# A fused Mamba-2 and Hadamard-FFN layer: the preparation stage's work moved into batch 0's own order

## What is computed

```python
xn = _layernorm(x)
# attention part: a Mamba-2 block on xn, and its own residual
zxbcdt = xn @ w_in                       # 512 -> z 1024, xBC 1280, dt 16
xBC = silu(causal_conv4(xBC) + conv_b)   # -> xh, B, C
y = ssd(xh * dt, dt * A, B, C) + xh * D  # state-space scan over the rows
y = y * silu(z)
y = y * rsqrt(mean(y * y) + EPS) * norm_w
mamba = xn + y @ w_out
# feed-forward part: gate, Hadamard transform of 2048, down
hidden = silu(xn @ W1.T) * (xn @ W3.T)   # 512 -> 2048
hidden = fwht(hidden)                    # / sqrt(2048)
ffn = hidden @ W2.T                      # 2048 -> 512
out = x + mamba + ffn
```

## Time and profile before

| | us |
|---|---|
| median of 3 runs | 1034.17 (1034.06 to 1037.31) |
| profiled execution | 1032.72 |
| its span, first to last instruction | 1030.8 |
| preparation, to the first projection | 0 to 111.3 |
| batch 0 | 111.3 to 357.9 |
| batches 1, 2, 3 | to 582, 806 and 1028 |

### The profile page before, as it was taken

How to read it: one execution, slowest core, us unless ns; L and a number is a source line. 1 busy time by engine, 2 the same in 40 slices (tenths; PEclk the granted TensorE clock), 3 DMA queues, 4 the chain that set the end, 5 groups by cost and what they waited for, 6 DMA issues and landing times.

```text
span 1030.8 us, 13120 instructions
## 1 busy us (share of the span) xinstructions
PE 925.2 (90%) x4924; PEld 464.5 (45%) x4926; DVE 649.1 (63%) x1096; ACT 384.1 (37%) x637; POOL 296.4 (29%) x182
## 2 busy tenths in 40 slices
PE   1027879998899999999999999999999999999997
PEld 1013334454454544555544444555544445555543
DVE  3997788778875275666754276766762565766631
ACT  3548455634432233623322234522321234442300
POOL 1962020434520020345410020544400111654400
PEclk9999899999999999999999999999999999999999
DMA  8448656754642153543622343643532433455123
GB/s 297 188 163 307 213 152 196 236 174 120 204 138 82 60 166 102 170 128 93 174 83 62 106 141 104 193 128 99 131 93 62 152 97 102 133 145 130 64 72 92
DMA packets 95103, 143.10 MB, mean 139 GB/s; under 512 B 7744, under 2 KB 46272, under 8 KB 91456
## 3 DMA queue, kind: packets, MB, share of 16 engines
q1 hardware_dynamic: 77120, 114.73, 36.2%
q10 hardware_dynamic: 17920, 27.53, 9.1%
HBM read 120.47 MB, written 21.76 MB: 138 GB/s over the span
## 4 chain that ended last, share of the span: by engine, by line
PE 76%; DVE 11%; DMA 5%; ACT 3%; issue 3%; SPq 1%; ACTq 0%; DVEq 0%
PE ps L434 49%; PE ps L592 16%; PE ps L564 3%; DMA arena<-w_in 2%; DMA arena<-w1t 2%; PE ps L550 2%; DVE arena L933 2%; DVE arena L348 2%; DVE arena L347 2%; PE ps L556 2%; PE ps L496 2%; PE ps L536 1%; DVE arena L973 1%; ACT arena L696 1%; PE ps L444 1%
## 5 line engine op out<-in xcount | busy, mean ns | idle before, releaser
L434 PE MATMUL ps<-xh,arena 128*128 128x512 f16 x1600 | 493.8, 383 | 15.5 <-DVE arena L973 9.0
L434 PE MATMUL ps<-xl,arena 128*128 128x512 f16 x800 | 306.5, 383 | 0.0
L434 PEld LDWEIGHTS ps<-xh,arena 128*128 128x128 f16 x1600 | 160.0, 100 | 207.2 <-issue 21.4
L1110 POOL TENSOR_TENSOR arena<-arena 128x512 f16<-128x512 f32 x64 | 82.5, 1290 | 317.5 <-ACT arena L736 317.5
L592 PE MATMUL ps<-arena 128*128 128x512 f16 x768 | 169.8, 379 | 0.0
L1116 POOL TENSOR_TENSOR arena<-arena 128x2048 f32<-128x2048 f32 x16 | 58.0, 3627 | 285.4 <-DMA arena<-cs_rows 285.4
L973 DVE SCALAR_TENSOR_TENSOR arena<-ps,cw,arena 128x511 f32<-128x511 f32 (+2 forms) x120 | 89.6, 749 | 52.0 <-ACT arena L726 50.1
L434 PEld LDWEIGHTS ps<-xl,arena 128*128 128x128 f16 x800 | 78.9, 99 | 89.3 <-issue 3.5
L592 PEld LDWEIGHTS ps<-arena 128*128 128x128 f16 x768 | 74.4, 98 | 88.0 <-issue 0.7
L736 ACT ACTIVATE arena<-arena 128x512 f16<-128x512 f32 x64 | 40.3, 630 | 167.8 <-DVE arena L994 167.8
L434 PE MATMUL ps<-wo_hi,arena 128*128 128x512 f16 x256 | 78.8, 379 | 0.0
(11 more groups left out here) (155 smaller groups left out, 1108.8 us busy)
## 6 DMA issues: line engine op xcount, KB each, us to landing
arena<-w_parts SPq DMA_DIRECT2D x214, 256.0 KB, 2.7
w_parts<-arena SPq DMA_DIRECT2D x66, 256.0 KB, 2.3
arena<-cs_rows ACTq DMA_DIRECT2D x16, 1024.0 KB, 6.0
arena<-ecs_rows ACTq DMA_DIRECT2D x24, 256.0 KB, 7.4
arena<-w_in SPq DMA_DIRECT2D x4, 1160.0 KB, 17.7
arena<-w_in SPq DMA_DIRECT2D x18, 256.0 KB, 3.7
arena<-x SPq DMA_DIRECT2D x4, 1024.0 KB, 6.5
arena<-w2t SPq DMA_DIRECT2D x1, 4096.0 KB, 16.4
```

The lines of the kernel that those rows point to most:

```text
L434: ins = nc.tensor.matmul(out_ap, lhs(i, a), rhs(i, c), start=(i == 0 and s == 0), stop=(i == n - 1 and s == 2))
L1110: nc.gpsimd.tensor_tensor(hid_lo[:, i, :], hs[i % 2], hid_hi[:, i, :], ALU.subtract).then_inc(hid_l.sem, 1)
```

## The change

There is no preparation stage. Each batch has its own order, and batch 0's holds what was prepared, as items of its own:

- `w_in`, W1 and W3 come from the host cut into tiles (each tile a contiguous block, in batch 0's order). All eighteen tiles of w_in are loaded once, at the start, into what is later the hidden buffers, and are split from there.
- The scale of w_in is two scales: one from the first four tiles and dt's columns, one (G1S) from the other fourteen.
- W1 and W3 are squared in four rounds: KA is the squaring (W1 on ACT, W3 on POOL, in four pieces each), K the column sum on PE and a maximum on DVE, KS the scale.
- W2 comes from the host with its rows shuffled, and the transform is two matmul passes: F with one sign matrix (16 matmuls, ACT squares the input and copies the result out, SP stores it as w2_mid) and, after the norm W2S, H with another (16 matmuls through PSUM bank 4, then split by ACT and DVE straight into the buffers from which G reads). W1's and W3's columns are shuffled alike. F stands between the up tiles, H between the last up tiles and the down tiles. W2's raw tiles lie in the hidden buffers.
- WOL, WOQ, WOS and WOH load, square, scale and split W_out, XL loads the next batch's x, HL starts the load of w2_mid.
- After w_in, raw tiles have six buffers in place of two (the two of before and the four buffers of W2's parts), and a load is issued eight tiles ahead.
- x of batch 0 is loaded first, in four pieces, and normalised by DVE. Constants are loaded from ACT's queue. A scale is four instructions in place of eight.
- The last chunk's N, V and W use bank 5 alone.

```diff
-RAW, PARTS, W2R = 2, 5, 4
+PARTS, W2R = 5, 4
+CONV_ORDER = [B_TILE, C_TILE] + list(range(QE))
+G1_PIECES = ((4, 8), (8, 12), (12, 16), (16, 18))
+RING = (("1", 0), ("3", 0), ("1", 1), ("3", 1), ("1", 2), ("3", 2), ("1", 3), ("3", 3))
+NRING = 5
+RAWS = 6
+RAW_LEAD = 8
+FIRST = ("B G1S C C0 DT C1 Z0 SUM C2 KA0 Z1 C3 K0 KA1 Z2 WOL C4 K1 KA2 Z3 C5 K2 KA3 Z4 C6 K3 KS Z5 C7 Z6 E0 Z7 F0 F1 "
+         "A0").split()
+FIRST_AT = ([("WOQ", q, q // 2 + 1) for q in range(8)] + [("WOS", 0, 6)] + [("WOH", q, q // 2 + 7) for q in range(8)] +
+            [("XL", 0, 14), ("HL", 0, 28), ("W2S", 0, 29)] +
+            [("F", m, 4 * (m // 2) - 2 + m % 2) for m in range(2, JF)] + [("H", j, 30 + j) for j in range(JF)])
...
         def load_raw(sp, p):
 
-            sp.wait_ge(w_lo.sem, w_lo.at(0, p - RAW))
-            sp.dma_start(raw[p % RAW], weight_tile(STREAM[p])).then_inc(d_raw[p % RAW], 16)
+            q = p - N_FRONT
+            if q >= RAWS:
+                sp.wait_ge(w_lo.sem, w_lo.at(0, p - RAWS))
+            elif q < 2:
+                sp.wait_ge(w_lo.sem, w_lo.at(0, q))
+            sp.dma_start(raws[q % RAWS].rearrange("p k m -> p (k m)"), weight_tile(STREAMS[0][p])).then_inc(d_raw[q % RAWS], 16)
...
+            for t in range(NC):
+                sp.dma_start(xraw[:, t, :], x[0, t * P:(t + 1) * P, :]).then_inc(d_x0[t], 16)
...
+                        if b == 0 and N_FRONT <= p + RAW_LEAD < NT:
+                            load_raw(sp, p + RAW_LEAD)
...
+                    elif kind == "H":
+                        if i + W2R < JF:
+                            load_h(sp, i + W2R)
+                        sp.wait_ge(evac.sem, evicted(0, (kind, i)))
+                        sp.dma_start(w2_parts[i].rearrange("p (a d) -> p a d", a=2), w2s[i % W2R]).then_inc(d_w2st[i % W2R], 16)
...
+                    elif kind == "G1S":
+                        pe.wait_ge(scale_g0, 1)
+                        pe.wait_ge(sq_g1, len(G1_PIECES))
+                        pe_norm(pe, SQ_G1, SQ_G1 + 5, sum_g1)
+                    elif kind == "K":
+                        pe.wait_ge(scale_g1, 1)
+                        pe.wait_ge(ones16_ok, 1)
+                        if i > 0:
+                            pe.wait_ge(k_read, i)
+                        pe.wait_ge(k_act, i + 1)
...
+                        pe.wait_ge(k_pool, 4 * (i + 1))
...
+                    elif kind == "F":
+                        to = claim((kind, i))
+                        pe.wait_ge(d_had, 16)
+                        pe.wait_ge(d_w2r[i // 2], 32)
+                        nc.tensor.matmul(to, had_a, w2_raw[i], start=True, stop=True).then_inc(f_done, 1)
...
+                    elif kind == "H":
+                        if i == 0:
+                            pe.wait_ge(scale_w2, 1)
+                        else:
+                            pe.wait_ge(evac.sem, evicted(0, ("H", i - 1)))
+                        pe.wait_ge(d_h[i % W2R], 16 * (i // W2R + 1))
+                        nc.tensor.matmul(bank(4), had_b, h_raw[i % W2R], start=True, stop=True).then_inc(h_done, 1)
...
+                    elif kind == "F":
+                        act.wait_ge(d_w2r[i // 2], 32)
+                        if i > 0:
+                            act.wait_ge(sq_w2, i)
+                        square(w2_junk, w2_raw[i], SQ_W2 + i, sq_w2)
+                        act.wait_ge(f_done, i + 1)
+                        if i == 0:
+                            act.wait_ge(xt_done.sem, xt_done.at(0, MC - 1))
+                        elif i >= 2:
+                            act.wait_ge(d_mid[i % 2], 16 * (i // 2))
+                        nc.scalar.activation(w2m[i % 2], tile_bank(0, (kind, i)), ACT.Copy).then_inc(f_out_ok, 1)
...
+                    elif kind == "WOQ":
+                        act.wait_ge(d_wo, 16)
+                        if i > 0:
+                            act.wait_ge(sq_wo, i)
+                        nc.scalar.activation(wo_junk, wo_raw[:, i, :], ACT.Square, scale=nw[:, i:i + 1],
+                                             accum_out=row_sq[:, SQ_WO + i:SQ_WO + i + 1]).then_inc(sq_wo, 1)
...
+                    elif kind == "H":
+                        dve.wait_ge(had_hi, i + 1)
+                        nc.vector.scalar_tensor_tensor(out=w2s[i % W2R][:, 1, :], in0=bank(4), scalar=f_had[:, 0:1],
+                                                       in1=w2s[i % W2R][:, 0, :], op0=ALU.mult, op1=ALU.subtract).then_inc(evac.sem, 1)
...
+                    elif kind == "KA":
+                        n = RING_AT["3", i]
+                        pool.wait_ge(d_ring[n % NRING], 16 * (n // NRING + 1))
+                        if i > 0:
+                            pool.wait_ge(k_sums, i)
+                        for s in range(4):
+                            piece = slice(s * TILE, (s + 1) * TILE)
+                            nc.gpsimd.tensor_tensor(sq_pool[:, piece], ring[n % NRING][:, piece], ring[n % NRING][:, piece],
+                                                    ALU.mult).then_inc(k_pool, 1)
```

More of the change, by code:

```diff
@@ L168, in build @@
         row = view(1)
-        yh, yl = cut(view(E // 2, FP16), QE), cut(view(E // 2, FP16), QE)
-        assert used[0] >= STAGED
-        raw = [cut(view(KD * P), KD) for _ in range(RAW)]
+        w2_junk = view(D // 2, BF16)
+        yh = cut(view(E // 2, FP16), QE)
+        yl_at = used[0]
+        yl = cut(view(E // 2, FP16), QE)
+        raw_at = used[0]
+        raw = [cut(view(KD * P), KD) for _ in range(2)]
         parts = [view(KD * P, FP16) for _ in range(PARTS)]
@@ L472, in _ @@
-            pe_dt_proj(pe, 0)
-            pe.wait_ge(sq_ok_w, SQ_WO)
-            nc.tensor.matmul(bank(2)[:, 0:KD], ones, row_sq[:, 0:SQ_W2], start=True, stop=True)
-            nc.tensor.matmul(bank(2)[:, KD:KD + QE], ones, row_sq[:, SQ_IN:SQ_WO], start=True, stop=True).then_inc(sums_w, 1)
-            pe_cumsums(pe, 0)
-            def column_sums(i):
-                for squares, done in ((sq_act, w13_sq_act), (sq_pool, w13_sq_pool)):
-                    pe.wait_ge(done, i + 1)
-                    for n in range(HF // L):
-                        ins = nc.tensor.matmul(bank(4 + n), ones16, squares[i % 2][:, n * L:(n + 1) * L],
-                                               start=(i == 0 and squares is sq_act),
-                                               stop=(i == KD - 1 and squares is sq_pool), skip_group_check=True)
-                ins.then_inc(w13_sums, 1)
@@ new lines, in _, with square @@
+            act.dma_start(hads[:], consts[:, 4 * P:6 * P]).then_inc(d_had, 16)
+            def square(junk, w, column, done):
+                nc.scalar.activation(junk, w, ACT.Square, accum_out=row_sq[:, column:column + 1]).then_inc(done, 1)
+            act.wait_ge(guards, 1)
+            nc.scalar.activation(first[:], row_sq[:, SQ_G0 + 3:SQ_G0 + 4], ACT.Square)
+            act.wait_ge(d_g0, 48)
+            square(sq_act[:, 0:2 * TILE], at(raw_at, 2 * TILE), SQ_G0, sq_g0)
+            act.wait_ge(sq_g0, 1)
@@ new lines, in _ @@
+            dve_ln(dve, steps, 0)
+            dve.wait_ge(ln_ok.sem, ln_ok.at(0, 0))
+            for t in range(NC):
+                nc.vector.tensor_scalar(xraw[:, t, :], xraw[:, t, :], rstd[:, t:t + 1], nmr[:, t:t + 1], ALU.mult,
+                                        ALU.add).then_inc(xn_ok.sem, 1)
+            dve.wait_ge(sum_g0, 1)
+            to_scale(IN0, bank(FREE_BANK)[:, 0:4], ALU.add)
+            dve.nop().then_inc(scale_g0, 1)
+            dve_xl(dve, 0, (0, 1))
+            steps.step(nc.vector.tensor_scalar(f_in[:], inv[:, IN0:IN0 + 1], 1 / XS, None, ALU.mult))
@@ new lines, in _, with split_lo @@
+            dve.wait_ge(steps.sem, k)
+            dve.nop().then_inc(scale_g0, 1)
+            dve_xl(dve, 0, (2, 3))
+            def split_lo(p):
+                dve.wait_ge(w_hi.sem, w_hi.at(0, p))
+                n = group(p)
+                nc.vector.scalar_tensor_tensor(out=part_lo[p % PARTS], in0=raw_tile(p), scalar=scl[:, n:n + 1],
+                                               in1=part_hi[p % PARTS], op0=ALU.mult, op1=ALU.subtract).then_inc(w_lo.sem, 1)
+            for p in range(AHEAD):
+                split_lo(p)
@@ L966, in finish @@
                         a = acc[n % 2]
[L967 removed]
+                        due = stream[p - 2] if p > 1 and stream[p - 2][0] == "C" else None
                         if due and C_ORDER[due[1]] == n - 2:
```

833 lines of the change are left out of this document (459 added, 374 removed).

## The result

The changed kernel takes 1007.74 us (median; 1006.74 to 1010.94) against 1035.22 for the kernel before on the same chip: a ratio of 0.9739, 95% interval 0.9706 to 0.9772. It is faster by 27 us, where the prediction had 48, and lies 1.7 us outside its range of 966 to 1006. The profiled execution has a span of 1004.9.

What follows compares the result with a forecast made beforehand. Later batches are bound by PE; winnable are the 111 us ahead of the first projection and part of batch 0's 24 excess. 19.0 + 9.9 + 73.6 + 137.0 + 70.2 + 672.9 = 982.6 span, 986 us measured; range 966 to 1006.

Steps and rivals of the forecast that it cites:

- Start and first tile: Kernel start to first projection, 19.0 us in place of 111.3; then first tile and PE's wait for the norm, 9.9.
- Second tile to T0: Batch 0 from second tile to its first chunk step: 73.6 us, with 6.0 of stalls and 2.5 for lower clock.
- T0 to G0: Batch 0 from first chunk step to first down tile: 137.0 us, of which 7.0 are stalls.
- I take 7.0, half of the 14.2 that this stage had over batch 1; ends 0 and 20: Stalls between batch 0's first chunk step and first down tile, with DVE and ACT late: 7.0 us.
- The work term: PE's work between batch 0's first chunk step and first down tile, without stalls: 130.0 us.
- Raw loads at nothing: Raw weight loads between first chunk step and first down tile cost nothing with six buffers; without that cover 24 us at most.
- Down tiles: Batch 0's down tiles: 70.2 us, from 51.6 before, 11.2 for thirteen H and 7.4 of waits.
- The wait at H7: In batch 0's down tiles PE waits 5.4 us, as the next batch's layer norm delays reading H6.
- the 2.0 at H8: In batch 0's down tiles, a further PE wait of 2.0 us, one H after the layer norm's wait.
- The rest: From the end of batch 0's down tiles to the end: same work in the same order, 672.9 us as before.
- batch 0 is bound by DVE and ACT: Rival, chance 0.20: in-order queues hold splits, evictions and F; stalls of 14 and 20 in two stages give 1007 us.

Runs made afterwards that it cites:

- the repeat: The changed kernel run once more with nothing altered: 1011.11 us, 0.9777 of the kernel before.
- the run with both causes out: Changed kernel with seven of eight W_out squares and splits left out and POOL's subtraction on a quarter of its columns in batch 0: 991.77 us, 0.958.
- the last run: Changed kernel with layer norm in pieces, W_out's squares and split at other places, W of the first chunk later, W_out's norm at place 7: 996.86 us, 0.9645.

## Why the prediction was wrong

- **Start and first tile**: right. First projection at 19.96 for 19.0, the second tile 9.1 later for 9.9, with the wait of 4.1 on ACT's squares that was named.
- **Second tile to T0**: 76.9 for 73.6. PE's idle time was 7.0 for 6.0, at the places named (dt chain 1.86, K0 2.46, K3 behind POOL 2.28), though K0 waited for ACT's square of W1 and not for POOL's, and K1 and K2 for nothing. Its work was 70.0 for 67.6, with a granted clock of 0.95.
- **T0 to G0**: the failed step is the term "I take 7.0, half of the 14.2 that this stage had over batch 1; ends 0 and 20". It measured 22.2 (152.2 less 130.0), or 23.8 in the repeat, beyond its far end. The work term was right: 129.9 in the run with both causes out. Its own argument named the first cause, ACT level with PE over the first four tiles, and then priced it by a share of another kernel's stalls. What the runs showed in its place has three parts. W_out's squares stand in a chain over ACT, DVE and PE at X0, so what counts is the longest path at one place and not the sum over four tiles: the gap at F is 4.35 with squares at places 1 to 4, 2.73 with none at place 3, 1.68 with one of eight left. W_out's low parts stand ahead of a reduce that PE waits for, and DVE's low splits and low parts don't go on beside POOL's subtraction. And the long gaps were paid again: of the 22.2, 6.0 is PE's work at the lower level, which the front's sum had (2.5 after its wait) and this one had not.
- **Raw loads at nothing**: right as a forecast, for no wait of ACT for w1 or w3 is in the profile. The price without the cover was too low, 24 for some 38. It was taken from a kernel without F, whose store now stands ahead of the raw load in SP's queue; that this is the difference isn't shown.
- **Down tiles**: 72.4 for 70.2. The wait at H7 is 5.26 for 5.4, on DVE's L1185 as named; the 2.0 at H8 did not come; 1.38 at the next batch's transposes, which was not in the sum, did, and the tile behind H7's gap ran at the lower level. The run with the layer norm elsewhere and the one with it in pieces confirm the cause.
- **The rest**: 674.3 for 672.9.
- **The rivals**: the time is that of "batch 0 is bound by DVE and ACT", 1007, but by its mechanism only in T0 to G0; it had 14 us of stalls in the front, where there were 7. As a bound by busy time it is refuted: 9 us less of ACT in the stage, or 6 less of DVE, moved nothing beyond the scatter. (DVE's part of that is weak, since only 6 of 19 us could be taken away.) Both engines are late at single places. The time near this rival's is in part luck for it: two stages were to be at their far ends, and one was, beyond it.

Left open: what each of the smaller gaps (2.15 to 3.0 us near 180, 1.41 at H1) is worth alone, how much of the two causes in T0 to G0 is POOL's hold on DVE and how much POOL's own chain, and how much of the scatter between executions comes from where POOL's and DVE's instructions happen to meet. POOL's other instructions were not shortened, though low splits met them too (2.06 us beside L1315 at 207.38).

## What to carry to other kernels

When prepared work is spread over a pipelined stage, price it at the place where it stands: follow the longest chain across engines through that place, and add the next work at the lower clock for each long gap: here those of 4.3 to 5.3 us were all followed by it, those of 2.5 to 3 us in part. Long steps belong where the other engines have slack in each turn and in pieces shorter than that slack; moving them whole only moved the wait. And before a DVE instruction is placed, look for the long POOL instruction that runs there.

## What the runs showed of the hardware that was not expected

- DVE instructions that read SBUF alone, some of them, went on only when POOL's beside them had ended, whatever their own size: a low split of 128x128 ended 0.15 us after POOL's in each of five cases in the run with short low splits (1.69 to 3.57 us long beside the subtraction; 0.33 at its shortest), one of 128x512 0.55 us after it (2.49 at 180.27; 0.75 alone), the scaling of 128x8 0.03 us after it (3.06; 0.22 in the kernel after). It isn't all of them: in the kernel before, DVE's instructions of 128x1 took 0.15 to 0.16 us in the middle of POOL's square at 73.63, and Q0's reduce took 1.96 us beside POOL's L1349 in the last run, 1.90 in the kernel after. DVE's eviction L1142, with one input in PSUM, stayed between 0.678 and 0.694 us in all its 64 executions. It goes the other way too: the subtraction takes 3.61 us, and 4.17 where a low split had begun 0.05 us ahead of it (at 178.05).
- How long PE stood still did not by itself tell whether its clock fell. The 2.46 us ahead of K0 in the kernel after and the 2.74 ahead of F in the last run were followed by the lower level at once (F took 1.90 in place of 1.02). After 2.96 us in the run without W_out's work and 2.82 in the repeated change, the tile behind ran at a granted clock of 1.00; after 2.87 us without the squares, the first matmuls took the full level's time and those from 1.1 us on the lower's. After 4.34, 4.68 and 5.26 us it was the lower level each time, and after 4.68 a tile took 5.24 in place of 2.6. In the kernel before, 2.22 us was not followed by it.
- A load of 256 KB from issue to landing, in the median: 9.2 us for the 26 raw loads of W1, W3 and W2 from 29 to 106 (272 GB/s), 3.0 for the 22 of T0 to G0 (179 GB/s), and 2.7 for a ready part. With six buffers ACT never waited for one; with two it waited 57.5 us, though the 27 of that stage landed in 3.4.
